# Attention and MoE on one core: an earlier residual of queries and keys, and the split of the maxima on GpSimd

## The chip, the cores and the metric

One of the eight cores of one Trainium2 chip runs the whole kernel. The metric is the device time of one execution in microseconds (us), smaller is better. In the texts and the profile PE is TensorE, DVE is VectorE, ACT is ScalarE, POOL is GpSimd and SP is SyncE, which here only issues DMAs.

## What is computed

```python
x = L0_attn_x                                   # (32, 256, 128)
xn = layernorm(x)
# attention: 16 heads of 8, causal, window of 64, rotary embedding
qkv = (xn @ Wqkv.T); q, k = rope(q), rope(k)
attn = softmax(where(allow, q @ k.T / sqrt(8), -inf))
y = (attn @ v) @ Wproj.T + bproj
# mixture of experts: 8 experts of width 512, the best 2 for each token
gates = xn @ gate_w.T + gate_b                  # top 2, softmax over them
out = sum_e w_e * (gelu(xn @ w1[e] + b1[e]) @ w2[e] + b2[e])
return x + y + out
```

Scores must come out as of float32, with 8 numbers to a head. So each rotated query and key is written as a sum of three bf16 parts (leading, middle, last), and the products of parts are laid along the contraction. The row maximum of the scores, which is subtracted before the exponential, is a sum of three bf16 parts as well: it enters the second score product as three more rows.

## The kernel before

**The order.** `schedule()` writes one list, `ORDER`, and every engine walks through it and takes its own part of each entry. So the order of `ORDER` is the order on each engine's queue, and an engine that waits at an entry holds back all later ones. Time is cut into quarters `q`; a batch `b` is one of 32 sequences of 256 tokens, four quarters each. The tables `middle` and `late` say, for each `q % 4`, which stages are put in, and with which distance: `("rest", 18)` does `rest` of batch `(q + 18) // 4`. In one quarter stand, in this order: `scoresT` (second score product and its exponential) of q, `pv` of q - 1, the stages of `middle`, `scores` (first score product on PE, its row maximum on DVE) of q + 10, the stages of `late`, then the normalisation and routing stages, then scatters of token rows.

**Queries and keys of batch b** go through `qk` (PE, quarter 4b - 22), `rope` (DVE, L977 to L982, 4b - 21), `add` (DVE, L988, 4b - 20), `turn_qk` (PE transposes into PSUM bank 6, L616, 4b - 20, late), `hi` (ACT, L1145: leading bf16 part, 4b - 19), `rest` (DVE, L995: the residual, PSUM minus leading part, 4b - 18), `mid` (ACT, L1150: middle part, 4b - 17), `lo` (POOL, L1247: last part, 4b - 16 late, and 4b - 17 late for b < 12), `write` (SP, L475 and L477: six DMAs to DRAM, 4b - 15 late, or 4b - 16 late for b < 12), `load` (SP, L488: four DMAs back in the layout `QK`, 4b - 13 late), and first `scores` (PE L632, L639) at 4b - 10. `write` waits for `lo`; `load` waits for the landing of `write` and for the second product of batch b - 4; `scores` waits for the landing of `load` and for the maximum before it (bank 0 and 1 are one buffer).

**The maxima of batch b**: four reductions on DVE (L1004), the last one in quarter 4b - 7, then in the same quarter, late, `msplit` on DVE: L1012, L1014, L1016, L1018, four operations on 128x32, each waiting for the one before it. `turn_m` (PE, L648) transposes them at 4b - 5 late (for b of 28 and more at 4b - 6), `mput` and `mget` (ACT) send them through DRAM, and `scoresT` needs them at 4b. Behind `msplit` on DVE comes `norm_y` (L1025, L1029) of the next quarter, for which PE waits in `turn_y` (L717), then `rest`, then the next maximum.

**POOL** otherwise issues the scatters of token rows to the experts' slots (L1292, an indirect DMA each, 128 of them in quarters 28 to 97, 1 to 3 to a quarter by `SPREAD`), each held until `scores` of its quarter is done; then, in the expert stage, the scatters of results (L1298), and at the end `combine` (L1303), which adds the two experts' rows once their fetch has landed and which DVE's own `combine` (L1080) waits for.

**The stages.** Quarters up to 104 are attention of batches 0 to 25 with the look-ahead of later ones, routing on DVE and POOL from quarter 18 on; then the 71 units of the experts run on PE; then come the last quarters with fetches and stores.

```python
    middle = ((("add", 20), ("out", -4), ("mput", 4), ("residual", -8)), (("hi", 19),),
              (("norm_y", -6), ("rest", 18), ("mget", 2), ("expand", 2)), (("rope", 21), ("mid", 17)))
```

Of the kernel before, what the change touches and what calls it, by code (L numbers as in the profile page):

```python
# [43 lines left out]
def schedule():  # L44
# [12 lines left out]
    middle = ((("add", 20), ("out", -4), ("mput", 4), ("residual", -8)), (("hi", 19),),  # L57
              (("norm_y", -6), ("rest", 18), ("mget", 2), ("expand", 2)), (("rope", 21), ("mid", 17)))
    late = ((("turn_qk", 20), ("lo", 16), ("write", 16)), (("turn_o", -5), ("msplit", 7), ("write", 15)),
# [126 lines left out]
def attention_moe_kernel(nc, x, wqkv, wproj, bproj, gate_w, gate_b, w1, b1, w2, b2, cf, cb, out):  # L186
# [3 lines left out]
    ALU = mybir.AluOpType  # L190
# [27 lines left out]
    with ctx:  # L218
# [6 lines left out]
        xn = xflat[:].rearrange("p (t c) -> p t c", c=W)  # L225
# [45 lines left out]
        mx = sb("mx", [P, 2, 32])  # L271
        mr = sb("mr", [P, 2, 32])
        ms = sb("ms", [P, 2, 96], bf16)
# [55 lines left out]
        def semaphore(name):  # L329
            return ctx.enter_context(nc.semaphore(name))  # L330
# [19 lines left out]
        e_xt, e_vg, e_rt, e_qk, e_qt, e_sc, e_mt, e_st = (semaphore("e_" + n) for n in (  # L350
            "xt", "values", "route", "qk", "qkT", "scores", "maxT", "scoresT"))
# [5 lines left out]
        v_rb, v_rc, v_rr, v_mx, v_ms, v_rd, v_ys, v_att = (semaphore("v_" + n) for n in (  # L357
            "rope_b", "rope", "rest", "max", "msplit", "recip", "y", "attention"))
# [7 lines left out]
        p_init, p_cb, p_nrm, p_xn, p_lo, p_b, p_cmb, p_rt, p_row = (semaphore("p_" + n) for n in (  # L366
            "init", "const", "norm", "xn", "lo", "bias", "combine", "route", "row"))
# [172 lines left out]
        def _(e):  # L540

            b4, b5, b6, b7 = [], [], [], []
            for what, *a in ORDER:
# [5 lines left out]
                elif what == "turn":  # L549
                    n = a[0]  # L550
# [9 lines left out]
                elif what == "vg":  # L560
                    n = a[0]
# [35 lines left out]
                elif what == "qk":  # L597
                    b = a[0]
# [10 lines left out]
                elif what == "turn_qk":  # L609
                    b = a[0]  # L610
# [9 lines left out]
                elif what == "scores":  # L620
                    b, t, c = a[0] // 4, a[0] // 2 % 2, a[0] % 2
# [21 lines left out]
                elif what == "turn_m":  # L643
                    b = a[0]
                    for sem, v in b5:
                        e.wait_ge(sem, v)
                    e.wait_ge(v_ms, 4 * b + 4)
                    e.transpose(ps[0:96, 5, 0:64].bitcast(bf16), ms[:, b % 2, :], identb).then_inc(e_mt, 1)  # L648
                    b5 = [(a_mt, b + 1)]
                elif what == "scoresT":  # L650
                    b, t, c = a[0] // 4, a[0] // 2 % 2, a[0] % 2
# [33 lines left out]
                elif what == "pv":  # L685
                    b, t, c = a[0] // 4, a[0] // 2 % 2, a[0] % 2
# [17 lines left out]
                elif what == "turn_o":  # L704
                    b = a[0]
# [7 lines left out]
                elif what == "turn_y":  # L713
                    b = a[0]
# [5 lines left out]
                elif what == "proj":  # L720
                    b = a[0]
# [50 lines left out]
        def _(e):  # L772
            nrm = 0
            e.memset(zer[:], 0.0).then_inc(v_init, 1)
            for what, *a in ORDER:
# [11 lines left out]
                elif what == "norm":  # L787
                    g = a[0]
                    u0, u1 = GR[NR[g]], GR[NR[g + 1]]
                    y, a_, b_ = nw[:, 0, u0:u1], nw[:, 1, u0:u1], rs[:, u0:u1]  # L790
# [31 lines left out]
                elif what == "vput":  # L822
                    n = a[0]
# [147 lines left out]
                elif what == "rope":  # L971
                    b = a[0]
# [10 lines left out]
                elif what == "add":  # L983
                    b = a[0]
# [4 lines left out]
                elif what == "rest":  # L989
                    b = a[0]  # L990
# [7 lines left out]
                elif what == "scores":  # L998
                    b, t, c = a[0] // 4, a[0] // 2 % 2, a[0] % 2
                    e.wait_ge(e_sc, a[0] + 1)  # L1000
                    if a[0] % 4 == 0 and b >= 2:
                        e.wait_ge(v_ms, 4 * (b - 2) + 2)
# [3 lines left out]
                elif what == "msplit":  # L1006
                    b = a[0]
                    s2 = b % 2
                    e.wait_ge(v_mx, 4 * b + 4)
                    if b >= 2:  # L1010
                        e.wait_ge(e_mt, b - 1)
                    e.tensor_copy(ms[:, s2, 0:32], mx[:, s2, :]).then_inc(v_ms, 1)  # L1012
                    e.wait_ge(v_ms, 4 * b + 1)
                    e.tensor_tensor(mr[:, s2, :], mx[:, s2, :], ms[:, s2, 0:32], ALU.subtract).then_inc(v_ms, 1)  # L1014
                    e.wait_ge(v_ms, 4 * b + 2)
                    e.tensor_copy(ms[:, s2, 32:64], mr[:, s2, :]).then_inc(v_ms, 1)  # L1016
                    e.wait_ge(v_ms, 4 * b + 3)
                    e.tensor_tensor(ms[:, s2, 64:96], mr[:, s2, :], ms[:, s2, 32:64], ALU.subtract).then_inc(v_ms, 1)  # L1018
                elif what == "norm_y":
                    b = a[0]  # L1020
# [188 lines left out]
        def _(e):  # L1209
# [7 lines left out]
            for what, *a in ORDER:  # L1217
# [25 lines left out]
                elif what == "lo":  # L1243
# [4 lines left out]
                                    sp[:, b % 2, :, 1, :], ALU.subtract).then_inc(p_lo, 1)  # L1248
                elif what == "route":
# [124 lines left out]
```

## Time and profile before

| | |
|---|---|
| median of 3 runs | 764.87 us (759.67 to 767.23) |
| span of the profiled execution, first to last instruction | 707.8 us |
| PE busy in it | 639.5 us (90%) |
| DVE busy | 480.9 us (68%) |
| ACT busy | 357.6 us (51%) |
| POOL busy | 371.5 us (52%) |
| mean granted clock of PE | 0.961 |

The span leaves out some 57 us before the first and behind the last instruction. The groups of rows below are to be read with two things in mind: a wait is idle time of the engine just before an instruction, with the instruction that ended it where the profile finds one ("issue" where it finds none); and an indirect DMA on POOL is followed by 0.30 us in which POOL shows no work even when its next instruction is ready.

### The profile page before, as it was taken

The numbers are of one execution on the slowest core, as the hardware profiler recorded it, in microseconds if no ns is written. First come the engines' busy times: TensorE is split into PE (matmuls) and PEld (weight loads), VectorE is DVE, ScalarE is ACT, GpSimd is POOL, SyncE is SP. The second block draws the span as 40 slices with busy tenths as digits, with TensorE's granted clock in tenths as the row PEclk, the third lists the DMA queues.
The fourth block names the chain that finished last, engine by engine and source line by source line (L and its number), as shares of the span: only waits on it lengthen the run. The fifth ranks groups of instructions, "written<-read, shape, count | busy, mean of one in ns | idle before, by whom it ended". The sixth has DMA issues, their size and how long they took to land.

```text
span 707.8 us, 26391 instructions
## 1 busy us (share of the span) xinstructions
PE 639.5 (90%) x10175; PEld 515.1 (73%) x10175; DVE 480.9 (68%) x1366; ACT 357.6 (51%) x681; POOL 371.5 (52%) x461
## 2 busy tenths in 40 slices
PE   7677999887989899899989899999999999999885
PEld 3455677655666567666667799999998999996653
DVE  6877797899888688879877344444444444446874
ACT  1354767544556466566556344444444444446552
POOL 1673352246667577777650444545454545453453
PEclk7698999999999999999999999999999999999997
DMA  8578768846878778777687867777777676784988
GB/s 257 180 199 233 207 188 222 221 141 188 252 215 238 218 208 227 217 210 210 193 224 225 249 198 247 237 239 238 242 239 235 225 253 226 251 236 110 312 255 261
DMA packets 156236, 157.92 MB, mean 223 GB/s; under 512 B 20224, under 2 KB 131096, under 8 KB 156112
## 3 DMA queue, kind: packets, MB, share of 16 engines
q1 hardware_dynamic: 141576, 135.29, 66.1%
q0 software_dynamic: 8416, 17.51, 7.2%
q10 hardware_dynamic: 6120, 3.43, 1.8%
q8 instruction: 82, 1.34, 0.8%
q14 instruction: 42, 0.34, 0.2%
HBM read 102.19 MB, written 58.61 MB: 227 GB/s over the span
## 4 chain that ended last, share of the span: by engine, by line
PE 63%; DVE 18%; DMA 8%; issue 6%; SPq 3%; POOL 1%; ACT 0%; ACTq 0%; DVEq 0%
PE ps L762 16%; PE ps L749 15%; DVE mx L1004 7%; PE ps L697 6%; PE ps L632 4%; PE ps L639 3%; PE ps L605 3%; PE ps L681 2%; PE ps L616 2%; DMA QK<-stack 2%; PE ps L725 2%; PE ps L735 2%; PE ps L674 2%; DMA xn<-slots_x 1%; PE ps L567 1%
## 5 line engine op out<-in xcount | busy, mean ns | idle before, releaser
L1298 POOL DMA_INDIRECT chosen_y<-xn,to x135 | 129.2, 957 | 136.4 <-DVE xn L1072 111.3
L1004 DVE TENSOR_REDUCE mx<-ps 128x8 f32<-128x1024 f32 x128 | 156.3, 1221 | 52.4 <-PE ps L639 51.9
L1205 ACT ACTIVATE hb<-ps,xn 128x256 f32<-128x256 f32 x284 | 113.2, 461 | 142.3 <-PE ps L749 142.2
L1183 ACT ACTIVATE PT<-ps 128x1024 f32<-128x1024 f32 x128 | 131.1, 1024 | 88.2 <-PE ps L681 88.1
L1292 POOL DMA_INDIRECT slots_x<-xn,pos x128 | 126.2, 986 | 57.8 <-issue 31.7
L762 PEld LDWEIGHTS ps<-xn,hb 128*128 128x128 f32 x1080 | 131.2, 192 | 3.9 <-ACT hb L1205 0.6
L762 PE MATMUL ps<-xn,hb 128*128 128x128 f32 x1080 | 132.1, 275 | 0.4 <-DVE xn L1066 0.4
L749 PE MATMUL ps<-xn 128*128 128x256 f32 (+1 forms) x568 | 130.1, 372 | 0.0
L749 PEld LDWEIGHTS ps<-xn 128*128 128x128 f32 x568 | 100.2, 192 | 10.3
L697 PE MATMUL ps<-PT,V 128*32 128x64 f32 (+1 forms) x3072 | 86.5, 246 | 1.7 <-ACT Os L1190 1.0
L1066 DVE TENSOR_TENSOR xn<-ps,xn 128x256 f32<-128x256 f32 x71 | 29.1, 410 | 83.3 <-PE ps L762 83.0
L632 PE MATMUL ps<-cb_s 64*64 64x512 bf16 x512 | 53.7, 408 | 20.0 <-issue 10.1
L697 PEld LDWEIGHTS ps<-PT,V 128*32 128x32 f32 x3072 | 58.0, 112 | 12.7 <-issue 1.9
L1247 POOL TENSOR_TENSOR sp<-rr,sp 128x512 bf16<-128x512 f32 x32 | 37.2, 1162 | 52.5 <-ACT sp L1150 52.1
L639 PEld LDWEIGHTS ps<-QK 48*64 48x64 bf16 x2048 | 46.9, 108 | 14.2 <-issue 2.9
L639 PE MATMUL ps<-QK 48*64 48x128 bf16 x2048 | 53.2, 219 | 1.2 <-issue 1.2
L681 PE MATMUL ps<-QK 51*128 51x64 bf16 (+1 forms) x1536 | 51.5, 200 | 0.0
L681 PEld LDWEIGHTS ps<-QK 51*128 51x128 bf16 x1536 | 44.6, 95 | 9.5 <-issue 0.5
L1057 DVE TENSOR_TENSOR to<-eq,cf_s 128x2 int32<-128x2 f32 x71 | 11.4, 161 | 52.4 <-DMA chosen_y<-xn,to 51.2
L632 PEld LDWEIGHTS ps<-cb_s 64*64 64x64 bf16 x512 | 15.5, 104 | 40.4 <-issue 36.2
L605 PE MATMUL ps<-wq_s,xnT 128*128 128x256 f32 x128 | 39.1, 431 | 3.0 <-ACT Vt L1114 2.6
L1303 POOL TENSOR_TENSOR xn<-xn 128x256 f32<-128x256 f32 x32 | 23.5, 751 | 27.6 <-DMA xn<-chosen_y 27.6
(151 smaller groups left out, 891.9 us busy)
## 6 DMA issues: line engine op xcount, KB each, us to landing
xn<-experts SPq DMA_DIRECT2D x71, 578.0 KB, 3.9
QK<-stack SPq DMA_DIRECT2D x128, 192.0 KB
stack<-sp SPq DMA_DIRECT2D x64, 192.0 KB
xn<-slots_x SPq DMA_DIRECT2D x64, 132.0 KB, 3.4
stack<-sp SPq DMA_DIRECT2D x64, 128.0 KB
xn<-chosen_y SPq DMA_DIRECT2D x32, 256.0 KB, 4.7
stack<-sp SPq DMA_DIRECT2D x64, 64.0 KB
Vc<-values SPq DMA_DIRECT2D x32, 128.0 KB
```

Of the source, the lines that this page charges most:

```text
L605: k = e.matmul(ps[:, 5, t * 256:(t + 1) * 256], xnT[:, c0:c0 + P], wq_s[:, 0:256], start=True, stop=True, skip_group_check=True)
L632: e.matmul(ps[q0:q0 + 64, g, :].rearrange("p (h k) -> p h k", h=4), unit[r:r + 64, 0:64], (win0 if t + blk == 0 else win)[r:r + 64, :].uns ...
L639: k = e.matmul(ps[q0 % P:q0 % P + m, g, h4 * P:(h4 + 1) * P], qk_rows(0, g, 48, s, hh, q0, m), qk_rows(1, g, 48, s, hh, w0, P), start=Fals ...
L681: k = e.matmul(ps[:, B + g, h4 * P + q0 % P:h4 * P + q0 % P + m], qk_rows(1, g, 51, s, hh, w0, P), qk_rows(0, g, 51, s, hh, q0, m), start= ...
L697: k = e.matmul(ps[32 * j:32 * j + 32, 4, o0:o0 + n], V[:, b % NV, w, 4 * g + j, 16 * c:16 * c + 32], PT[:, a[0] % 2, i0:i0 + n], start=t + ...
L749: k = e.matmul(ps[:, 2 * s + c // 2, (c % 2) * SL:(c % 2) * SL + m], w1b[:, i % NW, c * P:(c + 1) * P], xsT[:, i % 3, 0:m], start=True, st ...
L762: k = e.matmul(ps[:, bk, j * P:(j + 1) * P], hb[:, s, c, j * P:(j + 1) * P], w2b[:, i % NW, c * P:(c + 1) * P], start=c == 0, stop=c == 3, ...
L1004: e.tensor_reduce(mo[:, :, :, c, t], ps[:, 0:2, :].rearrange("p g (h k) -> p g h k", k=P), AX.X, ALU.max, negate=True).then_inc(v_mx, 1)
L1183: e.activation(PT[:, u % 2, :], ps[:, stb(u):stb(u) + 2, :].rearrange("p c k -> p (c k)"), ACT.Exp, scale=SCALE).then_inc(a_exp, 1)
L1205: e.activation(hb[:, s, c, 0:m], ps[:, 2 * s + c // 2, (c % 2) * SL:(c % 2) * SL + m], ACT.Gelu, bias=b1b[:, i % NW, c:c + 1]).then_inc(a_ ...
L1292: e.indirect_dma_start(out=Xs, out_offset=bass.IndirectOffsetOnAxis(ap=pos[:, n, u:u + 1], axis=0), in_=xn[:, u, :], in_offset=None).then_ ...
L1298: e.indirect_dma_start(out=Ys, out_offset=bass.IndirectOffsetOnAxis(ap=to[:, i % 4, j:j + 1], axis=0), in_=yb[:, i % 4, j, :], in_offset=N ...
```

## The change

`hi` goes from the middle of quarter 4b - 19 to the late part of 4b - 20, right behind `turn_qk`. `rest` goes from 4b - 18 to 4b - 19, `mid` from 4b - 17 to 4b - 18. `lo`, `write` and `load` stay where they are in the list. `msplit` is made on POOL, in the same place of the list, with the same four operations; those who waited for DVE's semaphore wait for POOL's (`turn_m`, and the maximum that overwrites `mx` two batches later).

```diff
-    middle = ((("add", 20), ("out", -4), ("mput", 4), ("residual", -8)), (("hi", 19),),
-              (("norm_y", -6), ("rest", 18), ("mget", 2), ("expand", 2)), (("rope", 21), ("mid", 17)))
-    late = ((("turn_qk", 20), ("lo", 16), ("write", 16)), (("turn_o", -5), ("msplit", 7), ("write", 15)),
+    middle = ((("add", 20), ("out", -4), ("mput", 4), ("residual", -8)), (("rest", 19),),
+              (("norm_y", -6), ("mid", 18), ("mget", 2), ("expand", 2)), (("rope", 21),))
+    late = ((("turn_qk", 20), ("hi", 20), ("lo", 16), ("write", 16)), (("turn_o", -5), ("msplit", 7), ("write", 15)),
             (("qk", 22), ("turn_y", -6)), (("lo", 17), ("vload", 5), ("load", 13), ("proj", -7), ("turn_m", 5)))
...
-                    e.wait_ge(v_ms, 4 * b + 4)
+                    e.wait_ge(p_ms, 4 * b + 4)
                     e.transpose(ps[0:96, 5, 0:64].bitcast(bf16), ms[:, b % 2, :], identb).then_inc(e_mt, 1)
...
                     if a[0] % 4 == 0 and b >= 2:
-                        e.wait_ge(v_ms, 4 * (b - 2) + 2)
+                        e.wait_ge(p_ms, 4 * (b - 2) + 2)
...
+                elif what == "msplit":
+                    b = a[0]
+                    s2 = b % 2
+                    e.wait_ge(v_mx, 4 * b + 4)
+                    if b >= 2:
+                        e.wait_ge(e_mt, b - 1)
+                    e.tensor_copy(ms[:, s2, 0:32], mx[:, s2, :]).then_inc(p_ms, 1)
+                    e.wait_ge(p_ms, 4 * b + 1)
+                    e.tensor_tensor(mr[:, s2, :], mx[:, s2, :], ms[:, s2, 0:32], ALU.subtract).then_inc(p_ms, 1)
+                    e.wait_ge(p_ms, 4 * b + 2)
+                    e.tensor_copy(ms[:, s2, 32:64], mr[:, s2, :]).then_inc(p_ms, 1)
+                    e.wait_ge(p_ms, 4 * b + 3)
+                    e.tensor_tensor(ms[:, s2, 64:96], mr[:, s2, :], ms[:, s2, 32:64], ALU.subtract).then_inc(p_ms, 1)
```

The last block stands in the GpSimd program behind `lo`; the same block, with `v_ms`, is removed from the VectorE program.

## Rows read from the trace of the kernel before

**Rows 1.** Busy time by engine and granted clock, stretches of 20 us

```profile
core 0: us, PE busy (x) PEld busy (x) DVE busy (x) ACT busy (x) POOL busy (x), PEclk, DMA share, GB/s
140.00:160.00 20.00, 16.85 (x402) 11.52 (x396) 19.62 (x44) 10.03 (x17) 9.33 (x11) 1.00 0.50 138
160.00:180.00 20.00, 15.06 (x361) 10.27 (x350) 17.33 (x43) 9.61 (x15) 10.47 (x10) 0.94 0.67 202
...
300.00:320.00 20.00, 19.42 (x506) 14.05 (x507) 15.91 (x29) 13.31 (x20) 15.12 (x16) 1.00 0.75 211
```

**Rows 2.** PE's waits from 140 to 200 us: total, times, longest

```profile
PE ps L616 <- DVE rc L988: 3.6, 3, 2.0
PE ps L717 <- DVE ys L1029: 3.4, 3, 2.0
PE ps L648 <- DVE rb L982: 2.5, 3, 1.2
```

**Rows 3.** PE's waits from 200 to 365 us

```profile
PE ps L632 <- issue: 6.6, 5, 3.3
PE ps L632 <- DMA QK<-stack: 2.4, 2, 1.6
...
PE ps L717 <- DVE ys L1029: 0.9, 1, 0.9
```

**Rows 4.** Chain of waits from one `lo` to its `scores`: start, duration

```profile
261.18 1.18 POOL sp L1247
...
270.45 4.90 DMA QK<-stack
```

**Rows 5.** Timeline of POOL: one `lo`, and the last scatter

```profile
304.43 1.17 POOL L1247 TENSOR_TENSOR sp<-rr,sp 128x512 bf16<-128x512 f32 x1
...
363.16 0.96 POOL L1292 DMA_INDIRECT slots_x<-xn,pos  x1 [0.30 <-issue]
```

**Rows 6.** POOL's waits from 200 to 365 us: total, times, longest

```profile
POOL slots_x L1292 <- issue: 27.1, 86, 3.2
POOL slots_x L1292 <- PE ps L639: 15.2, 17, 2.9
```

**Rows 7.** Timeline of DVE around one split: start, duration, idle time before

```profile
306.47 1.23 DVE L1004 TENSOR_REDUCE mx<-ps 128x8 f32<-128x1024 f32 x1 [1.10 <-PE ps L639]
307.74 0.25 DVE L1012 CAST ms<-mx 128x32 bf16<-128x32 f32 x1
...
308.57 0.35 DVE L1025 RECIPROCAL rd<-ps 128x32 f32<-128x32 f32 x1
```

**Rows 8.** Chain of waits, 54 to 61 us: start, duration

```profile
54.37 0.28 DVE ms L1012
...
55.98 1.87 SPq L438
...
61.08 4.53 DMA QK<-stack
```

**Rows 9.** Groups by line, small operations of POOL: busy, mean ns | idle before

```profile
L1228 POOL TENSOR_TENSOR nw<-nw 128x6 f32<-128x6 f32 (+2 forms) x18 | 4.1, 227 | 1.4
...
L1276 POOL COPY xn<-pw 128x64 f32<-128x64 f32 x1 | 0.3, 312 | 0.1
```

**Rows 10.** Timeline of SP: load of the experts' first slots

```profile
370.10 0.43 SPq L512 DMA_DIRECT2D xn<-slots_x  x1
```

**Rows 11.** Timeline of POOL: the experts' last scatter, and the last maxima's time

```profile
645.31 0.96 POOL L1298 DMA_INDIRECT chosen_y<-xn,to  x1 [0.30 <-issue]
...
673.47 3.05 POOL L1303 TENSOR_TENSOR xn<-xn 128x256 f32<-128x256 f32 x4 [0.20 <-DMA xn<-chosen_y]
```

**Rows 12.** Timeline of PE at the first and the last of the last maxima

```profile
646.71 0.22 PE L648 MATMUL ps<-cb_s,ms 128*96 128x128 bf16 x1
...
678.24 0.44 PE L717 MATMUL ps<-cf_s,ys 128*128 128x128 f32 x2 [2.33 <-DVE ys L1029]
```

**Rows 13.** Timeline of DVE, an operation of a split beside a busy POOL

```profile
350.05 1.78 DVE L1014 TENSOR_TENSOR mr<-mx,ms 128x32 f32<-128x32 f32 x1
```

**Rows 14.** Waits before `lo` over the whole span

```profile
POOL sp L1247 <- ACT sp L1150: 52.1, 11, 9.4
```

More of the change, by code:

```diff
@@ L356, in attention_moe_kernel @@
             "init", "bnstats", "stat", "norm", "xn", "gate", "route", "slots"))
-        v_rb, v_rc, v_rr, v_mx, v_ms, v_rd, v_ys, v_att = (semaphore("v_" + n) for n in (
-            "rope_b", "rope", "rest", "max", "msplit", "recip", "y", "attention"))
+        v_rb, v_rc, v_rr, v_mx, v_rd, v_ys, v_att = (semaphore("v_" + n) for n in (
+            "rope_b", "rope", "rest", "max", "recip", "y", "attention"))
         v_xs, v_to, v_wt, v_y, v_cmb, v_end, v_pos, v_tb = (semaphore("v_" + n) for n in (
@@ L364, in attention_moe_kernel @@
         a_exp, a_os, a_yt, a_gel = (semaphore("a_" + n) for n in ("exp", "out", "yT", "gelu"))
-        p_init, p_cb, p_nrm, p_xn, p_lo, p_b, p_cmb, p_rt, p_row = (semaphore("p_" + n) for n in (
-            "init", "const", "norm", "xn", "lo", "bias", "combine", "route", "row"))
+        p_init, p_cb, p_nrm, p_xn, p_lo, p_b, p_cmb, p_rt, p_row, p_ms = (semaphore("p_" + n) for n in (
+            "init", "const", "norm", "xn", "lo", "bias", "combine", "route", "row", "msplit"))
         block = ctx.enter_context(nc.Block())
@@ L1005, in _ @@
                                     ALU.max, negate=True).then_inc(v_mx, 1)
[L1006 to L1018, printed above, removed]
                 elif what == "norm_y":
```

## The prediction

> **What bounds the kernel now.** I read the busy times by stretch first. In the middle of the kernel PE is busy nearly always (19.42 of 20 us), but in the routing stretch, 140 to 200 us, it falls to 16.85 and 15.06 of 20 while DVE is busy 19.62 and 17.33 [rows 1]. There DVE sets the pace, and PE's waits name it: the rotated queries (L616), the normalised output (L717) and the rope that frees bank 5 (L648), 9.5 us in all [rows 2]. From 200 to 365 us PE waits for DVE hardly at all (0.9 us). What it waits for is the first score product, L632: 2.4 us put down to the load of `QK` and 6.6 us as "issue" [rows 3]. I take most of the 6.6 us as the same wait, since the instruction is the same. One instance shows the chain behind it: `lo` on POOL at 261.18, the issue of `write`, its landing, `load` at 270.45, and PE at 275.4, 14.2 us from the start of `lo` [rows 4]. The expert stage, 383 to 640 us, has neither split nor residual in it and stays as it is.
>
> Then I asked how full POOL is. A scatter takes 0.96 us with 0.30 us of idling before it, a `lo` 1.17 us and starts with no idling, so that the queue and not `mid` sets its time [rows 5]. From 200 to 365 us the two large rows of waits hold 27.1 + 15.2 = 42.3 us of idling before 103 scatters [rows 6]; 103 x 0.30 = 30.9 us are the scatters' own, so only 11.4 us of 165 are true idling. POOL, not DVE, is the second fullest queue there.
>
> **The part taken from DVE.** A split takes DVE from 307.74 to 308.57, 0.83 us [rows 7]. The 32 of them are 27 us, but they count only where DVE is last. In the routing stretch five splits stand, one to a batch of some 12 us, and DVE is full: 5 x 0.83 = 4.2 us gained. The upper bound is PE's 9.5 us of waits, the lower 2 us, if operations that wait for POOL's routing results come in the split's place. Further ahead, the first split stands in a chain over ACT and SP's store of the values, behind which the load of batch 2 is queued [rows 8]: 0.8 us there, and with a few more short waits 1.5 us for 45 to 140 us (0 to 4). From 200 us on the maximum before the split waits for PE 1.10 us anyway [rows 7], so DVE has slack and I take nothing.
>
> **The residual.** `rest` (0.68 us, as L995 before) now stands before the maximum of quarter 4b - 19, in that same 1.10 us of idling, and no longer before the next one. `hi` runs on ACT while PE makes the second product that ACT's exponential waits for. Both cost nothing; without that cover it would be 0.6 us a batch. What `mid` a quarter sooner gives is a sooner `lo`, where `lo` waits for `mid`. That is so for b < 12; there the loads are early enough but for batches 1 and 2, inside the 1.5 us. For b of 12 and more `lo` stays at 4b - 16 behind a scatter [rows 5]: no gain. `mget` is issued 0.6 us later, behind `mid`, with two quarters to land. SP's list is not changed: `write` is six DMAs, `load` four, each as before.
>
> **The part put on POOL.** No row shows these four operations on POOL. The nearest are small ones: 0.227 us and 1.4/18 us of idling, 0.31 us a step, at 6 to 12 elements, and 0.31 us with just under 0.1 before it, 0.39 us, at 64 [rows 9]. For 32 elements I take 0.34 us, 4 x 0.34 = 1.35 us (1.2 to 1.6). The Trainium skill, in "GPSIMD Engine Reference", section "Engine selection", puts two-input elementwise work on GpSimd at about twice VectorE's time, and so speaks against this move; by that rule a split would be 1.7 us and the shortfall worked out next 12 us instead of 7.5.
>
> From 200 to 365 us there are 14 splits: 14 x 1.35 = 18.9 us more for a queue with 11.4 us left. POOL falls 7.5 us short. When it is up to date it also has to wait for the maximum (1.23 us [rows 7]) before the split, with the quarter's scatters behind it. Who waits for POOL: `lo`, so `write`, so `load`, so PE at L632, a chain without slack, as PE waits there already [rows 3, 4]; `turn_m`, two quarters away; and the maxima two batches on. POOL's lag grows by some 0.5 us a batch, and once a microsecond of slack is used up PE takes POOL's pace. The last scatter ends at 364.1 [rows 5] and the experts' first slots are loaded at 370.1 [rows 10], so with some time to land a few microseconds are given back at the end. I take +8 us: the 7.5 and some waits for the maximum and idling that comes at the wrong place, less that room. The lower bound is 3 us, if slack at both ends hides the rest, the upper 18.9 us, if nothing is absorbed.
>
> **The last quarters.** The split of batch 28 stands on POOL behind the experts' last scatter, which ends at 646.3 [rows 11]. It would end near 647.6, and PE's transpose ran at 646.71 [rows 12]: +0.9 us. The splits of batches 30 and 31 hold back POOL's `combine`, which is back to back there [rows 11], and with it DVE's, which stands before `norm_y` and PE's L717, where PE already waits 2.33 us [rows 12]. Each adds 1.35 us of POOL and takes away 0.83 us of DVE, and one or two additions queue up behind it: +1 us each. That is 2.9; as the end hangs on fetches and stores too, I take +2 (0 to 4).
>
> **The sum.** -4.2 - 1.5 + 8 + 2 = +4.3 us on a span of 707.8, so 712.1. The median of the runs, 764.87, lies 57.1 us above the span; 764.9 + 4.3 = 769.
>
> **The rivals.** *POOL's work is paid in full* (slower). If the split waits for the maximum in most quarters, POOL's 11.4 us of idling are not used up but stay: 18.9 + 3 - 5.7 = +16 us, 781. For it: POOL must stand through a reduction that it did not wait for before. Against it: a POOL that lags finds the maximum ready.
>
> *POOL keeps up* (faster, so the other side). If its lag stays below the slack of the load, DVE's relief is what is left: -5.7 us, and over 1 us of the remaining L717 waits, -7 us, 758. It is decided by the start of `lo` against the end of its quarter's first product: a microsecond later than before, and it falls. For it: POOL's idling comes in lumps of up to 2.9 us [rows 6], in which a lag is lost. Also for it: an operation of DVE that reads two SBUF tensors took 1.78 us at 350.05, beside a scatter and a `lo` [rows 13], where the whole split is 0.83 us; such stalls would leave DVE. The Trainium skill has VectorE instructions with two SBUF inputs contend with GpSimd ("GPSIMD Engine Reference", section "Key points"); the trace agrees in this row. But it is one long stall of 1.6 us, at a place where DVE has over a microsecond of slack.
>
> *Nothing shows* (no change). DVE's gain in the routing stretch is lost in the routing's own exchanges with POOL, and POOL's lag is hidden: 765.
>
> **How the numbers follow.** Main case 0.50, 764 to 775, of which 0.06 lie above 772.5. Paid in full or near it 0.26, 773 to 783. Keeps up 0.15, 755 to 761. Nothing shows 0.09. A measurement of this kernel tells about 1% (7.6 us) from no change, so the bounds are 757.2 and 772.5. Slower: 0.26 + 0.06 = 0.32. Faster: 0.12, the larger part of the third case. Same: 0.56. For 8 in 10 the range runs from 757, which leaves out most of "keeps up", to 780, which leaves out the upper part of "paid in full".
>
> **What the profile would show.** Between 140 and 200 us PE's waits for DVE fall from 9.5 to about 5 us, and the stretch ends some 4 us sooner. From 200 to 365 us POOL shows its gaps of 0.30 us and few waits for PE L639; a split takes it 1.2 to 1.6 us; `lo` starts 2 us or more behind its quarter's product; PE waits over 15 us before L632 in place of 9.0. The idling before `lo` in the first batches (52.1 us [rows 14]) stays, ended by a `mid` that comes earlier. The prediction is wrong if POOL still waits 10 us or more for PE from 200 to 365 us with the last scatter issued before 363, or if a split on POOL takes under 1 us.

## The result, and the profile after

| | median, us | against the kernel before on the same chip |
|---|---|---|
| before | 764.51 (759.67 to 767.23) | |
| after | 796.22 (791.76 to 796.30) | 1.0421 (95% interval 1.0373 to 1.0469) |

The change costs 32 us, where +4.3 was forecast, and lies above the range. The profiled execution of after has a span of 794.5 us and a time of 796.3. That is the first surprise: in every run measured since, the span lies about 2 us below the time, while the 57 us between span and median were taken ahead of the prediction as time before the first and behind the last instruction. Those 57 us did not exist. The profiled execution of before (707.8 us) was of another speed than the three timed ones (765).

What differs came out with the repeats: the chips do. On some, called **the first kind** here (chips 7 and 4, and by its times the one of the result), the kernel before takes 765 to 769 us; on others, **the second kind** (chips 12, 13 and 15), the same kernel takes 712 to 716. The rows ahead of the prediction come from an execution as on the second kind. The three times it was set against look like the first. Each chip was met in one session only, so that it is the chip, and not something about the session, is not shown. In one table, with each kernel beside before on its own chip:

| kernel | first kind: us, ratio (interval) | second kind: us, ratio (interval) |
|---|---|---|
| before | 765.1 and 769.1 | 716.0, 711.6 and 712.0 |
| after | 796.2, 1.042 (1.037 to 1.047) | 724.1, 1.020 (1.011 to 1.029) |
| split on POOL alone | 792.7, 1.033 (1.024 to 1.042) | not run |
| sooner residual alone | 769.2, 1.007 (1.003 to 1.010), and 770.4, 1.000 (0.997 to 1.004) | not run |
| after, split behind its quarter's scatters | 772.0, 1.003 (0.999 to 1.006) | 725.7, 726.7 and 727.5: 1.014 to 1.024 |
| before, scatters joined, no work added | 804.5, 1.046 (1.042 to 1.051) | 722.2 to 722.9: 1.017 (1.006 to 1.028) and 1.018 (1.009 to 1.026) |
| before, POOL waits for the maximum | not run | 715.6 to 715.8: 1.004, 1.009 and 1.005 |
| before, four operations more on POOL | not run | 726.1 and 723.8: 1.016 and 1.017 |

**Where PE stands still.** The groups by line of after (busy, mean ns of one | idle before and what ended it):

```profile
PE 697.2 (88%) x10175; PEld 542.7 (68%) x10175; DVE 457.4 (58%) x1238; ACT 358.5 (45%) x681; POOL 403.4 (51%) x589
L697 PE MATMUL ps<-PT,V 128*32 128x64 f32 (+1 forms) x3072 | 103.4, 259 | 13.7 <-issue 12.0
L639 PE MATMUL ps<-QK 48*64 48x128 bf16 x2048 | 66.1, 234 | 21.6 <-issue 21.5
L1242 POOL CAST ms<-mx 128x32 bf16<-128x32 f32 x32 | 6.7, 209 | 110.0 <-DVE mx L1004 110.0
```

And before, run again on a chip of the first kind, the groups:

```profile
L697 PE MATMUL ps<-PT,V 128*32 128x64 f32 (+1 forms) x3072 | 96.1, 245 | 14.3 <-issue 11.5
L639 PE MATMUL ps<-QK 48*64 48x128 bf16 x2048 | 64.2, 222 | 16.1 <-issue 15.6
```

Beside this second profile of before (DVE 476.9 us, POOL 372.0), DVE gave up 476.9 - 457.4 = 19.5 us of work and POOL took on 403.4 - 372.0 = 31.4. But look at L639 and L697: they wait for nothing that the profile shows, and wait inside a product, 11.5 + 15.6 us already in before. I call these stops halts. In the profile that the prediction used, such waits come to 1.2 us at L639 and 0.4 us at L697 in the whole span. The last line of the first group is what is new in after: POOL stands 110 us, all told, before the split.

**What a halt looks like.** PE of after, 291.7 to 296.3 us (start, duration, idle before):

```profile
291.68 0.70 PE L697 MATMUL ps<-PT,V 128*32 128x64 f32 x14
292.80 0.31 PE L697 MATMUL ps<-PT,V 128*32 128x64 f32 x4 [0.41 <-issue]
293.51 0.22 PE L697 MATMUL ps<-PT,V 128*32 128x64 f32 x1 [0.40 <-issue]
...
294.25 0.38 PE L632 MATMUL ps<-cb_s 64*64 64x512 bf16 x1 [0.20 <-issue]
294.27 0.26 PE L639 MATMUL ps<-QK 48*64 48x128 bf16 x3
295.67 0.58 PE L639 MATMUL ps<-QK 48*64 48x128 bf16 x13 [1.03 <-issue]
```

POOL of after over the same time:

```profile
285.39 0.99 POOL L1292 DMA_INDIRECT slots_x<-xn,pos  x1 [0.17 <-issue]
288.78 0.21 POOL L1242 CAST ms<-mx 128x32 bf16<-128x32 f32 x1 [2.41 <-DVE mx L1004]
289.08 0.24 POOL L1244 TENSOR_TENSOR mr<-mx,ms 128x32 f32<-128x32 f32 x1
289.38 0.21 POOL L1246 CAST ms<-mr 128x32 bf16<-128x32 f32 x1
289.67 0.25 POOL L1248 TENSOR_TENSOR ms<-mr,ms 128x32 bf16<-128x32 f32 x1
290.07 1.01 POOL L1292 DMA_INDIRECT slots_x<-xn,pos  x1 [0.15 <-issue]
291.39 0.96 POOL L1292 DMA_INDIRECT slots_x<-xn,pos  x1 [0.30 <-issue]
292.65 0.96 POOL L1292 DMA_INDIRECT slots_x<-xn,pos  x1 [0.30 <-issue]
293.92 0.96 POOL L1292 DMA_INDIRECT slots_x<-xn,pos  x1 [0.31 <-issue]
```

Read the two together. POOL stands 2.41 us before the split; the two scatters behind the split are held back with it, and leave with those of the next quarter, four in one row from 290.07. PE's first halt begins at 292.4, 1 us after the second scatter began; it is the first of four, 2.0 us in all, of which the last ends at 295.67, 0.8 us after the last scatter of the row. The granted clock over 8 us each (busy by engine, then PEclk, in after):

```profile
284.00:292.00 8.00, 8.00 (x181) 5.57 (x177) 6.06 (x9) 4.87 (x9) 4.71 (x9) 0.92 0.54 159
292.00:300.00 8.00, 5.91 (x93) 3.87 (x94) 2.41 (x4) 2.46 (x3) 5.41 (x6) 0.72 0.56 142
300.00:308.00 8.00, 8.00 (x179) 5.62 (x171) 5.91 (x9) 4.27 (x8) 3.50 (x8) 0.86 0.51 148
```

In the trace the granted clock falls to 0.5 (1.2 GHz) at 295.44, during the last halt, and is back at 1.0 (2.4 GHz) at 302.27. Such a row comes about once a batch. Over 200 to 365 us, after and then before run again:

```profile
200.00:365.00 165.00, 139.92 (x2669) 93.83 (x2666) 88.19 (x125) 69.89 (x105) 98.85 (x129) 0.86 0.56 159
```

```profile
200.00:365.00 165.00, 141.89 (x3012) 96.22 (x3013) 107.93 (x192) 78.95 (x118) 99.28 (x99) 0.97 0.65 178
```

With two levels, a mean clock of 0.86 is 0.28 x 165 = 46 us at half clock, 0.97 is 0.06 x 165 = 10 us. In the same 165 us PE gets through 2669 matmuls instead of 3012, with nearly the same busy time: each takes longer, and it is not for want of work that they are fewer.

**By stage.** I cut every trace at the first maximum of batch 11, the first of batch 27, and the end of the expert products; the third stage therefore begins with the last 22 us or so of attention. Halts are idle times of PE over 0.15 us between two matmuls of one line:

| us | to batch 11 | batch 11 to 27 (halts: times, us; at half clock) | from batch 27 to the end of the experts | last quarters |
|---|---|---|---|---|
| before, second kind (rows above) | 183.8 | 180.7 (3, 1.6; 6.8) | 277.1 | 66.1 |
| after, second kind | 179.5 | 189.4 (1, 0.2; 18.7) | 283.2 | 73.3 |
| before, first kind | 183.2 | 222.2 (59, 22.6; 10.2) | 282.8 | 71.6 |
| after, first kind | 178.0 | 254.2 (68, 32.7; 78.5) | 286.5 | 75.8 |

The middle stage of before, run again, and of after, in one view:

```profile
183.20:405.40 222.20, 191.36 (x4085) 128.90 (x4083) 149.35 (x271) 107.06 (x162) 134.01 (x133) 0.98 0.65 177
178.00:432.20 254.20, 216.58 (x4081) 144.32 (x4080) 139.28 (x207) 107.50 (x161) 151.11 (x198) 0.85 0.55 158
```

On the first kind the middle stage alone has grown by 32.0 us, as much as the median time: PE's busy time by 25.2 us, for the same matmuls, and its idle time by 6.8. PE runs 68.3 us longer at half clock there. If all of it were paced by PE, that would cost half of it, 34 us (an estimate), more than the busy time grew; so not all of it is, and how the 32 us divide between the clock and the longer halts is not taken apart. The same stage holds most of the difference between the kinds, 222.2 - 180.7 = 41.5 of 52 us of span. The idle time understates the stops, since the matmul before a stop is still counted as busy during a part of it. From start to start, the steps of over 0.5 us between two matmuls of one line come to 2.8 us (4 of them) in before on the second kind, 40.6 (62) on the first, and 55.0 (74) in after on the first.

### The profile page after: what moved, and what is told of

It is laid out like the page before. It is cut to its first block, busy times and chain, and to the rows that moved or that the text cites. A ratio compares the mean times of both kernels' runs of the same rounds, so it can differ in the third digit from the quotient of the medians.

```text
span 794.5 us, 26391 instructions
## 1 busy us (share of the span) xinstructions
PE 697.2 (88%) x10175; PEld 542.7 (68%) x10175; DVE 457.4 (58%) x1238; ACT 358.5 (45%) x681; POOL 403.4 (51%) x589
## 4 chain that ended last, share of the span: by engine, by line
PE 62%; issue 7%; DMA 5%; DVE 4%; SPq 2%; ACT 1%; POOL 1%; another core or an unknown queue 1%; POOLq 0%; ACTq 0%; DVEq 0%
PE ps L762 13%; PE ps L749 12%; PE ps L697 8%; PE ps L632 5%; PE ps L639 4%; PE ps L681 3%; PE ps L725 3%; PE ps L605 3%; DMA xn<-slots_x 2%; PE ps L674 2%; PE ps L670 2%; PE ps L616 2%; PE ps L735 2%; DVE mx L1004 2%; PE ps L710 1%
## 5 line engine op out<-in xcount | busy, mean ns | idle before, releaser
L1292 POOL DMA_INDIRECT slots_x<-xn,pos x128 | 128.3, 1002 | 63.7 <-PE ps L639 34.7
L762 PEld LDWEIGHTS ps<-xn,hb 128*128 128x128 f32 x1080 | 132.0, 193 | 9.1 <-ACT hb L1192 4.7
L762 PE MATMUL ps<-xn,hb 128*128 128x128 f32 x1080 | 133.4, 276 | 4.9 <-ACT hb L1192 3.9
L697 PE MATMUL ps<-PT,V 128*32 128x64 f32 (+1 forms) x3072 | 103.4, 259 | 13.7 <-issue 12.0
L697 PEld LDWEIGHTS ps<-PT,V 128*32 128x32 f32 x3072 | 67.5, 120 | 31.1 <-issue 22.0
L639 PE MATMUL ps<-QK 48*64 48x128 bf16 x2048 | 66.1, 234 | 21.6 <-issue 21.5
L639 PEld LDWEIGHTS ps<-QK 48*64 48x64 bf16 x2048 | 51.8, 116 | 43.9 <-issue 34.9
L632 PE MATMUL ps<-cb_s 64*64 64x512 bf16 x512 | 66.0, 431 | 10.2 <-DVE mx L1004 3.7
L1242 POOL CAST ms<-mx 128x32 bf16<-128x32 f32 x32 | 6.7, 209 | 110.0 <-DVE mx L1004 110.0
L681 PEld LDWEIGHTS ps<-QK 51*128 51x128 bf16 x1536 | 49.1, 101 | 13.7 <-issue 3.0
L681 PE MATMUL ps<-QK 51*128 51x64 bf16 (+1 forms) x1536 | 56.8, 210 | 1.9 <-issue 1.9
L632 PEld LDWEIGHTS ps<-cb_s 64*64 64x64 bf16 x512 | 17.4, 106 | 38.3 <-issue 34.6
## 6 DMA issues: line engine op xcount, KB each, us to landing
xn<-chosen_y SPq DMA_DIRECT2D x32, 256.0 KB, 5.0
```

What stands on the lines that cost most here:

```text
L632: e.matmul(ps[q0:q0 + 64, g, :].rearrange("p (h k) -> p h k", h=4), unit[r:r + 64, 0:64], (win0 if t + blk == 0 else win)[r:r + 64, :].uns ...
L639: k = e.matmul(ps[q0 % P:q0 % P + m, g, h4 * P:(h4 + 1) * P], qk_rows(0, g, 48, s, hh, q0, m), qk_rows(1, g, 48, s, hh, w0, P), start=Fals ...
L681: k = e.matmul(ps[:, B + g, h4 * P + q0 % P:h4 * P + q0 % P + m], qk_rows(1, g, 51, s, hh, w0, P), qk_rows(0, g, 51, s, hh, q0, m), start= ...
L697: k = e.matmul(ps[32 * j:32 * j + 32, 4, o0:o0 + n], V[:, b % NV, w, 4 * g + j, 16 * c:16 * c + 32], PT[:, a[0] % 2, i0:i0 + n], start=t + ...
L762: k = e.matmul(ps[:, bk, j * P:(j + 1) * P], hb[:, s, c, j * P:(j + 1) * P], w2b[:, i % NW, c * P:(c + 1) * P], start=c == 0, stop=c == 3, ...
L1292: e.indirect_dma_start(out=Xs, out_offset=bass.IndirectOffsetOnAxis(ap=pos[:, n, u:u + 1], axis=0), in_=xn[:, u, :], in_offset=None).then_ ...
```

## The experiments

The theory after the result: **joined scatters**. The wait for the maximum that the split brings to POOL holds back a quarter's scatters, they leave in a row with the next ones, PE halts several times on end, and its clock falls. The rival is **POOL's work**, which the prediction had: four more operations a batch make POOL late.

**Before, run again; and the two parts of the change apart** (first kind, chip 7). `before_again` is the kernel before, unchanged. `pool only` is the second hunk onward of the change with the table of before; `order only` is the table of after with the split on DVE:

```diff
-              (("norm_y", -6), ("rest", 18), ("mget", 2), ("expand", 2)), (("rope", 21), ("mid", 17)))
-    late = ((("turn_qk", 20), ("lo", 16), ("write", 16)), ...
+              (("norm_y", -6), ("mid", 18), ("mget", 2), ("expand", 2)), (("rope", 21),))
+    late = ((("turn_qk", 20), ("hi", 20), ("lo", 16), ("write", 16)), ...
```

> The kernel before, unchanged. Its profiled execution spanned 707.8 us against a median of 764.9, while the changed kernel's profile spans 794.5 against 796.2. If the profile read ahead of the prediction was of an uncommon, fast execution, the span is now 758 to 766 and shows PE halting inside its score and value products (gaps of 0.4 to 1.3 us put down to issue, in one quarter of each batch) as the changed kernel does, 38.6 us of them there. If something else lies around the span, it is 708 again.

Measured 763.54 us, ratio 0.9996 (0.9954 to 1.0037), profiled span 759.8 us. So the profile adds nothing to the time, and the 57 us are a difference between executions of different speed.

> The split of the maxima on GpSimd, the order of hi, rest and mid as before. Theory of POOL's queue: the whole loss is here, 790 to 800 us. Rival, the order carries the loss: 760 to 770, or less, since DVE is relieved.

Measured 792.73 us, ratio 1.0327 (1.0236 to 1.0419); the middle stage is 251.7 us, with 75.1 at half clock.

> hi, rest and mid a quarter sooner, the split of the maxima left on VectorE. Theory of POOL's queue: no loss, 757 to 767. Rival, the order carries the loss (ACT's leading part stands between turn_qk and the next exponential, DVE's residual ahead of a maximum): 785 to 800.

Measured 769.24 us, ratio 1.0067 (1.003 to 1.0104), middle stage 226.1. The split alone costs 27.6 us by the medians and the order alone 4.1; together that is the 31.7 of the change.

**Wait and work apart** (second kind). `wait only` is before with one line on POOL, in the place of the split; `work only` is before with the four operations on POOL, on tiles of their own that nobody reads, and without the wait, while DVE keeps its split:

```diff
+                elif what == "msplit":
+                    e.wait_ge(v_mx, 4 * a[0] + 4)
```

> The kernel before; at the place of the split POOL waits for the batch's last maximum and does nothing (DVE makes the split as before). Theory of the joined scatters: a wait alone joins the scatters of two quarters into one row, so most of the loss of 29 us is here, 780 to 792, with PE at the lower clock for over 50 us of the scatter stretch. Theory of POOL's work: no loss, 762 to 769.

> The kernel before, with four more operations on POOL at the place of the split, of the same kinds and sizes on tiles that nobody else uses, chained as the split's but with no wait for the maximum. Theory of the joined scatters: 762 to 772. Theory of POOL's work (the prediction's): nearly the whole loss, 785 to 795.

Measured: `wait only` 715.65 us, 1.0038 (0.9988 to 1.0088); on two more chips of this kind 715.83, 1.0092 (1.0043 to 1.0140), and 715.57, 1.0049 (1.0000 to 1.0097). `work only` 726.07 us, 1.0161 (1.0071 to 1.0252), and 723.76, 1.0171 (1.0087 to 1.0256). On this kind it is the work that costs, +10 to +12 us, and the wait costs 0 to 7. In the second run of `work only` PE waits 12.7 us before the first score product from 200 to 365 us, against 9.0 in before.

**The split behind the scatters.** `split behind` is the kernel after with the split moved behind its quarter's scatters in the list, so that its wait holds back none of them:

```diff
-    late = (..., (("turn_o", -5), ("msplit", 7), ("write", 15)),
+    late = (..., (("turn_o", -5), ("write", 15)),
...
+        if q % 4 == 1 and 0 <= (q + 7) // 4 < NP:
+            order.append(("msplit", (q + 7) // 4))
```

> The changed kernel with the split on POOL behind the scatters of its quarter and no longer ahead of them, so the scatters of that quarter leave before the wait for the maximum. Theory of the joined scatters: 762 to 773, PE's halts single again. Theory of POOL's work: 790 to 797, as the work and its wait are the same.

Measured on the second kind: 725.72 us, 1.0140 (1.0064 to 1.0216); again 726.68, 1.0233 (1.0139 to 1.0326), and 727.49, 1.0244 (1.0135 to 1.0353). Nothing is won there, as hardly anything had been held back: from 200 to 365 us POOL of after waits 1.0 us for the maxima on this kind, once.

**Scatters joined without work or wait.** `joined` is before with other shares of the scatters for the four quarters of a batch:

```diff
-SPREAD = (1.0, 1.7, 2.6, 2.1)
+SPREAD = (1.0, 0.0, 4.3, 2.1)
```

> The kernel before with SPREAD (1.0, 0.0, 4.3, 2.1) in place of (1.0, 1.7, 2.6, 2.1): the same number of scatters to a batch, those of the second quarter moved into the third. Nothing else is on POOL. Theory of the joined scatters: 785 to 805, PE halting several times in one quarter and the clock at its lower level for over 50 us of the stretch. Theory of POOL's work: 762 to 769.

Measured on the second kind: 722.23 us beside 715.97 for before (no interval); again 722.85, 1.0166 (1.0056 to 1.0276), and 722.24, 1.0177 (1.0092 to 1.0261). Here rows of six and more scatters leave with hardly a halt (2 in the middle stage of the third run). In before on this kind there were already 15 rows of four and more, of up to eight scatters. What `joined` costs there, 6 to 12 us, I have not taken apart.

**After, on the second kind.**

> The changed kernel once more. In the comparison before last the kernel before took 765 us and PE halted inside its products during the scatters; in the last one, on another chip, it took 716 and PE did not halt. On a chip of the first kind: 792 to 800, PE at the lower clock for 70 to 80 us of the scatter stretch. On one of the second kind, by the prediction's own sum: 4 us over before, and with the additional POOL work seen to cost 10 us there, 716 to 728, with more waits at the first score product (9 us before) and no halts.

Measured 724.07 us, 1.0199 (1.0107 to 1.0292): +12.5 us, not 32. So the size of the loss depends on the kind of chip, and the theory of joined scatters, which is about the first kind, could only be tried there.

**The four kernels again, on chips 13 and 15.** Both chips turned out to be of the second kind, so these runs only repeat the results above (715.83 and 715.57 for `wait only`, 726.68 and 727.49 for `split behind`, 722.85 and 722.24 for `joined`, 723.76 for `work only`) and tell the theories apart no further.

> POOL only waits for the maximum. On the kind of chip where PE halts: theory of the joined scatters 780 to 792, theory of POOL's work 762 to 769. On the other kind 716, as before.

> The split on POOL behind the quarter's scatters. On the kind of chip where PE halts: theory of the joined scatters 762 to 775, theory of POOL's work 790 to 797. On the other kind 726, as before.

> The scatters of the second quarter of a batch moved into the third, nothing else on POOL. On the kind of chip where PE halts: theory of the joined scatters 785 to 805, theory of POOL's work 762 to 769. On the other kind 722, as before.

> The kernel before, whose POOL waits in each split's place for the batch's last maximum and does none of the split. Of the two chips met so far, one takes 764 us for the kernel before (its PE halts inside products while scatters leave in rows, and the whole change cost 32 us there), the other 712 to 716 us (nearly no halts, change 12.5 us). This kernel has run on the second chip only: 1.004 and 1.009. On a chip like the first: theory of joined scatters (the wait holds back a quarter's scatters, they leave in one row with the next quarter's, PE halts and its clock falls): 780 to 800 us, ratio 1.02 to 1.045, PE's mean granted clock under 0.93. Theory of POOL's work (the added operations make the halts worse): 762 to 770, ratio within 1%. On a chip like the second both say 1.00 to 1.01 again.

> The kernel after, whose split stands behind its quarter's scatters on POOL instead of ahead of them, so that the wait for the maximum holds back none of that quarter's. On a chip like the first (before 764): theory of joined scatters 768 to 780, ratio 1.005 to 1.02, the 12 us of POOL's work or less; theory of POOL's work 790 to 800 as the change itself, ratio 1.035 to 1.045. On a chip like the second (before 712 to 716): 1.014 to 1.023 again by both.

> The kernel before with the scatters' shares of the quarters changed from 1.0, 1.7, 2.6, 2.1 to 1.0, 0.0, 4.3, 2.1: no scatter behind the split's place, and four in a row a quarter later. No work and no wait is added. On a chip like the first: theory of joined scatters 780 to 800, ratio 1.02 to 1.045; theory of POOL's work within 1% of before. On a chip like the second 1.009 to 1.017 again.

> The kernel before with the four operations of a split done on POOL as well, on tiles of their own, without the wait for the maximum; DVE keeps its split. On a chip like the first: theory of joined scatters 766 to 778 (POOL's queue alone, as on the second chip), ratio 1.005 to 1.018; theory of POOL's work 785 to 800, ratio over 1.025. On a chip like the second 1.012 to 1.02 again by both.

**The two that decide, on the first kind** (chip 4, before 769.11):

> The kernel after, whose split stands behind its quarter's scatters on POOL. Measured on the second chip alone so far (727.49 us, 1.0244). On a chip like the first (before 764): theory of joined scatters 768 to 780, ratio 1.005 to 1.02; theory of POOL's work 790 to 800, ratio 1.035 to 1.045. On a chip like the second: 1.014 to 1.025 again.

> The kernel before with the scatters' shares 1.0, 0.0, 4.3, 2.1. Measured on the second chip alone so far (722.24 us, 1.0177). On a chip like the first: theory of joined scatters 780 to 800, ratio 1.02 to 1.045; theory of POOL's work within 1% of before. On a chip like the second 1.009 to 1.018 again.

`split behind` 771.96 us, 1.0025 (0.9992 to 1.0058): all of POOL's added work, and no loss that can be measured. The wait for the maximum is still in the program, but from 200 to 365 us POOL no longer stands in it (25.5 us in after): the scatters ahead of the split take up that time. `joined` 804.47 us, 1.0464 (1.0422 to 1.0506): no work, no wait, and more than the whole loss of the change. Both fall as joined scatters has it, `joined` even above its 780 to 800 and `split behind` below its ratio of 1.005; POOL's work falls on this kind. POOL of `joined` around one row, then of `split behind` (its L1293 is L1292 in after):

```profile
285.60 0.96 POOL L1292 DMA_INDIRECT slots_x<-xn,pos  x1 [3.91 <-PE ps L639]
286.87 0.96 POOL L1292 DMA_INDIRECT slots_x<-xn,pos  x1 [0.30 <-issue]
...
290.65 0.96 POOL L1292 DMA_INDIRECT slots_x<-xn,pos  x1 [0.30 <-issue]
293.68 0.95 POOL L1292 DMA_INDIRECT slots_x<-xn,pos  x1 [2.08 <-PE ps L639]
```

```profile
281.19 1.01 POOL L1293 DMA_INDIRECT slots_x<-xn,pos  x1 [0.15 <-issue]
282.50 0.96 POOL L1293 DMA_INDIRECT slots_x<-xn,pos  x1 [0.30 <-issue]
283.77 0.96 POOL L1293 DMA_INDIRECT slots_x<-xn,pos  x1 [0.30 <-issue]
286.56 0.96 POOL L1293 DMA_INDIRECT slots_x<-xn,pos  x1 [1.83 <-PE ps L640]
```

Their stretches from 200 to 365 us, `joined` and then `split behind`:

```profile
200.00:365.00 165.00, 138.39 (x2582) 94.55 (x2574) 92.86 (x171) 67.62 (x102) 84.82 (x84) 0.80 0.55 155
```

```profile
200.00:365.00 165.00, 140.97 (x2968) 95.32 (x2963) 97.67 (x140) 76.96 (x115) 109.19 (x144) 0.95 0.65 176
```

The clock, 0.80 and 0.95, goes with the rows, not with POOL's busy time (84.82 and 109.19). Counted over the traces of the first kind, a row being scatters less than 0.5 us apart (before and split on POOL alone are of chip 7, split behind and joined of chip 4, the two of the residual one of each; there is no trace of before on chip 4):

| first kind | rows of four or more | halts in the middle stage, and in such rows | at half clock, us | middle stage, us |
|---|---|---|---|---|
| before | 1 | 59, 5 | 10.2 | 222.2 |
| sooner residual alone, twice | 1 and 1 | 63, 4 and 67, 4 | 20.5 and 17.1 | 226.1 and 225.7 |
| split behind | 1 | 70, 6 | 27.3 | 228.8 |
| split on POOL alone | 17 | 65, 61 | 75.1 | 251.7 |
| after | 17 | 68, 62 | 78.5 | 254.2 |
| joined | 17 | 51, 51 | 99.0 | 259.7 |

In the middle stage no halt followed a single scatter, and none began before the second scatter of its row. The number of halts changes little (51 to 70); what changes is that they mostly come three to five together, and half clock follows. `wait only` and `work only` were not run on this kind. That the wait alone would join the rows is therefore inferred: from POOL's timeline above, and from 17 rows in place of 1 in both kernels whose split stands ahead of the scatters.

**The sooner residual once more**, on the same chip 4:

> The change's first part alone: hi, rest and mid a quarter sooner, the split still on DVE. On the first chip it was 769 us, ratio 1.0067. On a chip like the second: if the sooner residual costs and gives nothing there, as my prediction has it, within 0.5% of before and the whole 12.5 us of the change are POOL's part; the rival, that DVE's rest and ACT's hi in their new places hold up the maxima or the exponentials, gives 1.005 to 1.015 and leaves POOL's part half of the cost.

Measured 770.42 us, 1.0003 (0.9969 to 1.0038). This chip was of the first kind, so the share of the residual in the 12.5 us of the second kind stays open; on the first kind the medians of the two runs lie 1 and 4 us above before. Where such a cost would come from is shown below, under the experts.

## Why the prediction was wrong, point by point

**The failed step is the ground it stood on.** "The median of the runs, 764.87, lies 57.1 us above the span" was taken as time outside the span and added as a constant. Timed and profiled executions were simply different: the profile of before was of an execution in which PE hardly halts (3 times in the middle stage). A span 7.5% below the time ought to have been asked about first. With it fell everything that depended on how full POOL is: at 765 us PE is slower by its halts, and POOL has room (from batch 12 to 27 `lo` starts before its quarter's first score product has ended, in the median by 0.8 us in before and 1.1 us in after), as POOL's waits from 200 to 365 us show in before, run again:

```profile
POOL slots_x L1292 <- PE ps L639: 45.9, 34, 2.5
```

against 15.2 in [rows 6]. A POOL that is ahead does meet the maximum before it is made. In after, first kind, same stretch:

```profile
POOL ms L1242 <- DVE mx L1004: 25.5, 10, 3.4
```

The prediction saw this wait ("it also has to wait for the maximum ... with the quarter's scatters behind it") and priced it as part of +8 us, by the time that POOL loses. What it did was not to delay POOL but to bunch scatters, and the price was paid by PE, in longer halts and at half clock, which the sum had at nothing. No rival had that mechanism; "paid in full" (781) had the wait, with the wrong payer.

**The mechanism it described is there on the second kind**, the one of its rows. POOL and PE of after on that kind, 200 to 365 us:

```profile
PE ps L632 <- issue: 9.2, 7, 2.1
PE ps L632 <- DMA QK<-stack: 6.4, 4, 3.1
```

```profile
POOL slots_x L1292 <- issue: 26.5, 95, 1.6
POOL slots_x L1292 <- PE ps L639: 3.8, 8, 1.8
POOL ms L1242 <- DVE mx L1004: 1.0, 1, 1.0
```

- *PE waits over 15 us before L632 in place of 9.0*: 9.2 + 6.4 = 15.6. Right.
- *Few waits of POOL for PE L639, gaps of 0.30 us*: 3.8 against 15.2. Right. *`lo` starts 2 us or more behind its quarter's product*: 3.2 us in the median of batches 12 to 27, 0.7 in before. Right. And the maximum is nearly always ready when a late POOL comes to the split (1.0 us, once), as was said against "paid in full".
- *A split takes POOL 1.2 to 1.6 us*: from the end of the scatter before it to the start of the next 1.31 us, of which 0.15 still stand before that scatter. The estimate was 1.35. Right, and 1.6 times the 0.83 us of DVE. The two CASTs take 0.22 and 0.21 us on POOL and took 0.25 and 0.18 on DVE, the two subtractions 0.24 each on POOL and 0.19 on DVE. The Trainium skill ("GPSIMD Engine Reference", "Engine selection") puts GpSimd at about twice VectorE's time for operations with two inputs only, and near VectorE's rate for those with one. The prediction doubled all four and came to 1.7 us. For one input the trace agrees; for two inputs it shows a factor of 1.3 at 128x32, not two. The timeline of POOL, after, second kind:

```profile
307.10 0.98 POOL L1292 DMA_INDIRECT slots_x<-xn,pos  x1 [0.17 <-issue]
308.09 0.22 POOL L1242 CAST ms<-mx 128x32 bf16<-128x32 f32 x1
...
308.99 0.24 POOL L1248 TENSOR_TENSOR ms<-mr,ms 128x32 bf16<-128x32 f32 x1
309.39 1.01 POOL L1292 DMA_INDIRECT slots_x<-xn,pos  x1 [0.15 <-issue]
...
368.58 1.01 POOL L1292 DMA_INDIRECT slots_x<-xn,pos  x1 [0.15 <-issue]
```

- *+8 us for POOL's shortfall*: the middle stage grew by 189.4 - 180.7 = 8.7 us, and the last scatter starts at 368.58 against 363.16 [rows 5]. Right in size, and `work only` gives +10 to +12 us for the work without DVE's relief. The growth is 6.3 us of PE's idle time and 2.4 us of its busy time, with 18.7 us at half clock in place of 6.8. The 30.9 us taken as the scatters' own were too many: the 0.30 us stand only before a scatter that follows another one (0.17 behind `lo`, and the first operation of a split starts 0.01 us behind a scatter), so POOL had about 13.7 us of true idling where 11.4 were counted.
- *-5.7 us ahead of it*: 183.8 to 179.5, -4.3; on the first kind 183.2 to 178.0, -5.2. PE's waits for DVE from 140 to 200 us fall from 9.5 [rows 2] to 4.5 (about 5 was said):

```profile
PE ps L616 <- DVE rc L988: 1.7, 3, 1.0
PE ps L648 <- DVE rb L982: 1.6, 2, 0.9
...
PE ps L717 <- DVE ys L1016: 1.2, 1, 1.2
```

- Each part alone seems to bring some of it on the first kind: batch 11 is reached at 181.2 and 180.0 with the order alone, at 181.4 with the split on POOL alone, at 183.2 before. The prediction had given the residual nearly nothing. But `wait only`, which relieves nobody, also reaches batch 11 at 181.3 to 182.1 on the second kind, where before has 183.8, so 2 us between single traces prove little.
- *The idling before `lo` stays (52.1 us)*: wrong. In after on either kind 0.7 us are left. On the first kind the order alone leaves 39.6 and 39.8 of 57.1 us, as `mid` comes sooner, and the split on POOL alone 21.6, as POOL now waits before the split instead.
- *+2 us in the last quarters*: 66.1 to 73.3, so +7 against the execution that was read. But that one was short: `wait only` has 69.8 to 71.9 and `joined` 65.6 to 69.1 on the same kind, and beside them it is +1 to +8. On the first kind it is 71.6 to 75.8, +4, but the order alone has 76.4 and 77.0 and the split on POOL alone 76.7: either part brings it, and both together bring no more. The term's cause is not shown. Behind 645 us PE waits 9.2 us for `norm_y` in after on the second kind and 6.7 in before, but 9.1 also in before on the first kind.
- *`hi` costs nothing, and the expert stage stays as it is*: wrong at one place. The stage from batch 27 on grows from 277.1 to 283.2, +6 us, and from 282.8 to 286.5 on the first kind; with the order alone it is 284.1 and 285.2, with the split on POOL alone 282.3. From the first product of the experts' second layer (L762) on it takes 254.5 and 256.0 us on the second kind, 261.1 and 260.8 on the first. What grows is the time before it, 22.6 to 27.2 us and 21.7 to 25.7. In the list of before, `hi` of batch 31 stands behind the experts; a quarter sooner, it stands ahead of their first gelu on ACT, and it has to wait for the landing of `write` of batch 29, whose tile it overwrites. ACT's table load and the gelus wait behind it, and PE behind them. Before, then after on the second kind:

```profile
382.43 1.28 ACT L1205 ACT_TABLE_LOAD   x1 [0.38 <-ACT mT L1158]
```

```profile
392.59 0.60 ACT L1132 ACTIVATE sp<-ps 128x512 bf16<-128x512 f32 x1 [5.00 <-DMA stack<-sp]
393.20 1.28 ACT L1192 ACT_TABLE_LOAD   x1
396.12 1.29 PE L762 MATMUL ps<-xn,hb 128*128 128x128 f32 x7 [3.32 <-ACT hb L1192]
```

PE's wait at this place is 3.3 us here, 3.5 in after on the first kind, 2.6 and 2.4 with the order alone; in both traces of before and with the split on POOL alone it is absent. It is the one cost of the sooner residual that the traces show, and the prediction's sum had no term for it.

So for the kind of its own rows the sum said +4.3 and +12.5 was measured (ratio 1.011 to 1.029). The stages of the two traces differ by 17.7 us (-4.3, +8.7, +6.1, +7.2), more than the medians do, as the execution of before was a short one; of the sum's terms, the wait for `hi` was missing and the last quarters were too small. The 32 us of the result are another thing, joined scatters on the first kind.

## What to carry to other kernels

Before a sum is made, set the profiled execution's span against the timed runs: a gap of more than a few microseconds means that another execution was profiled than was timed, and waits read from it may not be the ones that are paid. When work with a wait of its own is moved to a queue that also issues transfers, ask what the wait does to their spacing, not only to their time: here, on the first kind, putting the split behind the scatters instead of ahead of them took the cost from 4.2% to nothing that can be measured. When an operation is moved up by one place in a rolling schedule, look at the edges of the schedule too: for the last batch the place was in front of another stage. None of the versions measurably beat the kernel before on either kind of chip.

## What the hardware showed that was not expected

- The same kernel takes 712 to 716 us on three chips and 765 to 769 on two; 41.5 of the 52 us of span lie in the middle stage, where PE makes short stops inside products (59 of them against 3; counted from start to start, steps of over 0.5 us come to 40.6 us against 2.8).
- On the slower kind, no stop follows a single indirect DMA on POOL in the middle stage. From the second of a back-to-back row on, in the median 1.0 to 1.1 us after its start, PE stops for 0.15 to 1.2 us. On the other kind rows of six to eight pass nearly without (3 stops in the stage). Why the kinds differ, and what PE lacks when it stops, is not known: the transfers on the queue of instructions last as long on both (1.2 to 1.3 us in the mean in the middle stage, before and after), so slow fetches of that kind are not shown as the cause.
- Where the stops come one to three together the clock mostly stays up (10 us at half in the middle stage of before, 59 stops; 17 to 27 us in the other kernels with one row of four or more); three to five on end are mostly followed by 1.2 GHz (75 to 99 us in all, in the kernels with 17 such rows). That the halts bring the clock down is read from this order of events, and no run changed the one without the other.
- Four dependent operations on 128x32 take POOL 1.3 us and DVE 0.83 us, of which POOL's operations themselves are 0.21 to 0.25 us each; the rest is about 0.08 us between them and 0.15 us before the next scatter.
